# Latent cross-attentions: each slot's side work on PE in front of the transposes of the probabilities

## The chip, the cores and the metric

The kernel runs on one core of one Trainium2 chip. The metric is the device time of one execution in microseconds. The engines are called by their short names: PE (TensorE, matmuls and transposes), DVE (VectorE), ACT (ScalarE), POOL (GpSimd) and SP (SyncE). PSUM, in which PE's results land, has 8 banks of 128 x 512 float32.

## The reference

A decoder of four layers on x of 4 batches x 512 tokens x 256 features, float32. Each layer has an attention, a cross-attention and a feed-forward part. The change touches three of the four cross-attentions, those of layers 1, 2 and 3, in which the tokens are the latents that ask, and keys and values come from 64 context rows and from the tokens themselves. That of layer 2, cut to what matters:

```python
def _L2_xattn_ref(x, latents, mask, ...):      # HEADS = 16, DIM_HEAD = 64
    xn = layernorm(x, ln_x_g, ln_x_b)          # x: the context, 64 rows
    ln = layernorm(latents, ln_l_g, ln_l_b)    # latents: the tokens, 512 rows
    q = (ln @ Wq).reshape(b, m, h, d).transpose(0, 2, 1, 3)
    kv = jnp.concatenate([xn @ Wkv, ln @ Wkv], axis=1)
    kv = kv.reshape(b, n + m, 2, h, d)
    k = kv[:, :, 0].transpose(0, 2, 1, 3)
    v = kv[:, :, 1].transpose(0, 2, 1, 3)
    qn = rmsnorm(q, qn_g) * scale
    kn = rmsnorm(k, kn_g)
    sim = jnp.einsum('bhid,bhjd->bhij', qn, kn)
    sim = jnp.where(padded_mask[:, None, None, :], sim, max_neg)
    attn = jax.nn.softmax(sim.astype(jnp.float32), axis=-1).astype(sim.dtype)
    out = jnp.einsum('bhij,bhjd->bhid', attn, v)
    return out.transpose(0, 2, 1, 3).reshape(b, m, h * d) @ Wout + bout
```

Layer 1 has no rmsnorm, mask or bias and 16 heads too. Layer 3 has 8 heads, l2-normed queries and keys, a mask, and a layer norm behind the output projection.

## The kernel before, in words

The program is one after the other twelve stages, written engine by engine; each engine runs its own list of instructions in the order of the code, and semaphores are the only link between lists. The stages of layers 1, 2 and 3 that matter are one function, `latent_attention` (line 2158), called three times. Nothing in it is planned by a program: the order is written out by hand.

**Slots.** For each batch `b` of four, the engines run a loop over slots `s`. A slot is one tile of 128 tokens (t = s % 4) of one pair of heads (j = s // 4): 32 slots in a batch with 16 heads, 16 with 8 heads. Slot s computes these things, each on its engine:

- PE waits for the exponentials of the slot before and makes the scores, 128 x 576 for each of the two heads, into PSUM banks 0 to 3 (line 2463).
- DVE adds the mask where there is one (L2826), takes the negated row maxima of the two heads (L2830), copies the transposed probabilities of slot s - 2 out of PSUM (`copy_probs`, L2760, one copy for each head), does small work for the next batch, and at the start of the next slot's list inverts the sums (`invert`, L2751).
- ACT makes the exponentials with their sums (L2588), then moves results of side work and of the pair out of PSUM (L2546, L2551, L2557, L2561).
- POOL scales the probabilities by the inverted sums (`share`, L2630 for the two heads' 512 tokens, L2633 for the context part).
- PE transposes the scaled probabilities of slot s - 2 (LAG = 2), four 128 x 128 blocks for each head, into bank 4 or 5 in turn (`turn_probs`, L2392). In slots with s % 4 = 1 it also transposes the context part of a whole pair into one of the same two banks (`turn_context_probs`, L2404), and in slots with s % 4 = 2 and 3, from s = 6 on, it multiplies the transposed probabilities of a pair with the values (`attended`, L2422, L2425).

**Side work.** `units_at(b, s)` gives PE at most one further unit in a slot; all units write bank 7. `value` (L2327, 4 matmul instructions) projects a tile of values of this batch; `out_part` (L2339, 8 instructions) is half of an output projection of a tile of the batch before (in layer 3 a whole one); `turn_batch` (L2319, 4 transposes) turns the next batch's normed rows. For 16 heads the values sit at s = 0 to 5, 8, 9, 12, 13, the outputs at s = 16, 17, 20, 21, 24, 25, 28, 29 of batches 1 to 3, and the turns at 26 and 27; for 8 heads the values at 0 to 4, the outputs at 5, 8, 9, 12 and the turns at 14 and 15 (`norm_units`, line 2142). `bank_free` holds the waits of a unit for bank 7.

**The waits that matter.** `turn_context_probs` waits for POOL and for `copied` of 8q + 7 (q counts the pairs): DVE's copy of the first head of slot s - 2, whose transposes stand in this same slot and used the bank that the context transposes write:

```python
n = 9 * q + 8
pe.wait_ge(shared, 3 * (b * NS + s) + 3)
pe.wait_ge(copied, 8 * q + 7)
```

`turn_probs` waits for POOL's scaling of its slot and for the earlier copy out of each bank. ACT's exponentials of slot g wait for the transposes of slot g - 3 (three buffers of probabilities).

Between two batches there is a tail, in which the last transposes are mixed with the projections of queries and keys of the next batch; its code is not touched.

Of the kernel before, what the change touches and what calls it, by code (L numbers as in the profile page):

```python
# [2157 lines left out]
def latent_attention(k, pre, H, names, unit=None, mask=None, bias_row=None, gain_row=None, offset_row=None):  # L2158
# [16 lines left out]
    LAG = 2  # L2175
# [7 lines left out]
    with ExitStack() as st:  # L2183
# [38 lines left out]
        def units_at(b, s):  # L2222

            out = []
            if s in VALUES:
                out.append(("value", VALUES.index(s)))
            if s in OUTS and b >= 1:
                out.append(("out", OUTS.index(s)))
            if s in TURNS and b + 1 < B:
                out.append(("turn", TURNS.index(s)))  # L2230
            return out
# [18 lines left out]
        def units_before(b):  # L2250
            return N0 + b * NQ

        with signals(nc, "ctx_stat", "ctx_aggr", "ctx_shift", "ctx_rstd", "ctx_normed", "ctx_turned", "ctx_ready",
# [28 lines left out]
            def _(pe):  # L2282

                def bank_free(b, s, kind):

                    if kind == "value":
                        n = VALUES.index(s)
                        if n:
                            pe.wait_ge(value_moved, b * NV + n)
                            if n % (TT + 1) == 0:  # L2290
                                pe.wait_ge(ctx_value_moved, b * A + n // (TT + 1))
                    if kind == "out":
                        n = OUTS.index(s)
                        if n % PER_OUT:
                            return
                        if n == 0:
                            pe.wait_ge(value_moved, b * NV + NV)
                            pe.wait_ge(ctx_value_moved, b * A + A)
                        elif TURNS[-1] > OUTS[n - 1] and TURNS[-1] < s and b + 1 < B:
                            pe.wait_ge(norm_moved, KC * (b + 2))  # L2300
                        else:
                            pe.wait_ge(out_added, TT * (b - 1) + n // PER_OUT)
                    if kind == "turn":
                        n = TURNS.index(s)
                        if n:
                            pe.wait_ge(norm_moved, KC * (b + 1) + n)
                        else:
                            before = sum(o < s for o in OUTS)
                            if b >= 1:
                                pe.wait_ge(out_added, TT * (b - 1) + before // PER_OUT)  # L2310
                            else:
                                pe.wait_ge(value_moved, b * NV + NV)
                                pe.wait_ge(ctx_value_moved, b * A + A)

                def turn_batch(b, c):
                    if c == 0:
                        pe.wait_ge(normed, TT * (b + 1))
                    for t in range(TT):
                        last = pe.transpose(k.ps[:, 7, t * P:(t + 1) * P], xr[:, t, c * P:(c + 1) * P], k.ident[:, :])  # L2319
                    last.then_inc(norm_turned, 1)  # L2320

                def value(b, n):
                    t, a = n % (TT + 1), n // (TT + 1)
                    for c in range(KC):
                        rows = xT[:, c, t * P:(t + 1) * P] if t < TT else \
                            ctx2[:, c, b, :, :].rearrange("p s n -> p (s n)")
                        last = pe.matmul(k.ps[:, 7, :], rows, wkv[:, c, W + a * 512:W + (a + 1) * 512],  # L2327
                                         start=c == 0, stop=c == KC - 1)
                    last.then_inc(value_made, 1)
# [45 lines left out]
                def step(i, i0, i1):  # L2375
                    if i < i1:
                        project(i)
                    if unit and i0 <= i - 2 < i1:
                        turn_unit(i - 2)

                def turn_probs(b, s):
                    q, t = b * PAIRS + s // 4, s % 4
                    for h in range(2):
                        n = 9 * q + 2 * t + h
                        pe.wait_ge(shared, 3 * (b * NS + s) + 1 + h)
                        if n % 9 == 1 and q >= 1:
                            pe.wait_ge(ctx_copied, q)
                        elif n >= 2:
                            pe.wait_ge(copied, 8 * q + 2 * t + h - (2 if n % 9 >= 2 else 1) + 1)
                        at = 0 if h == 0 else T + 2 * NC  # L2390
                        for c in range(TT):
                            last = pe.transpose(k.ps[:, 4 + n % 2, c * P:(c + 1) * P],  # L2392
                                                prob[:, (b * NS + s) % PB, at + c * P:at + (c + 1) * P], k.ident[:, :])
                        last.then_inc(prob_turned, 1)
# [51 lines left out]
                for b in range(B):  # L2446
                    for s in range(NS):
                        g = b * NS + s
                        if s == 0:
                            if unit:  # L2450
                                pe.wait_ge(moved, units_before(b + 1))
                            else:
                                pe.wait_ge(act_moved, units_before(b + 1) // 2)
                                pe.wait_ge(dve_moved, units_before(b + 1) // 2)
                            pe.wait_ge(placed, 2 * (b + 1))
                        else:
                            pe.wait_ge(exped, 2 * g)
                        j, t = s // 4, s % 4
                        for a in range(2):
                            for h in range(2):  # L2460
                                r = slice(64 * h, 64 * h + 64)
                                k0 = (NC if h == 0 else 0) + a * HALF
                                last = pe.matmul(k.ps[:, 2 * h + a, 0:HALF], qT[r, b % 2, j, t * P:(t + 1) * P],  # L2463
                                                 kT[r, j, k0:k0 + HALF], start=True, stop=True)
                        last.then_inc(scored, 1)
                        if s >= LAG:
                            turn_probs(b, s - LAG)
                        for kind, n in units_at(b, s):
                            bank_free(b, s, kind)
                            if kind == "value":  # L2470
                                value(b, n)
                            elif kind == "out":
                                out_part(b - 1, n, 7)
                            else:
                                turn_batch(b + 1, n)
                        if s >= LAG:
                            turn_context_probs(b, s - LAG)
                        if s >= 4 + LAG and (s - 4 - LAG) % 4 < 2:
                            attended(b, (s - 4 - LAG) // 4, (s - 4 - LAG) % 4)
                    i0, i1 = units_before(b + 1), units_before(b + 2) if b + 1 < B else units_before(b + 1)  # L2480
                    turn_probs(b, NS - 2)
                    if b + 1 < B:
                        pe.wait_ge(norm_moved, KC * (b + 2))
                        pe.wait_ge(exped, 2 * NS * (b + 1))
                        if b:
                            pe.wait_ge(out_added, TT * b)
                        for i in range(i0, i0 + 3):
                            step(i, i0, i1)
                    turn_probs(b, NS - 1)
                    if b + 1 < B:  # L2490
                        step(i0 + 3, i0, i1)
                    turn_context_probs(b, NS - 1)
                    if b + 1 < B:
                        for i in range(i0 + 4, i0 + 6):
                            step(i, i0, i1)
                    attended(b, PAIRS - 1, 0)
                    attended(b, PAIRS - 1, 1)
                    if b + 1 < B:
                        for i in range(i0 + 6, i1 + 2):
                            step(i, i0, i1)  # L2500
# [2424 lines left out]
```

## Time and profile before

| what | value |
|---|---|
| median of 3 runs | 3956.74 us (3950.29 to 3959.68) |
| the profiled execution, its own time | 3976.31 us |
| its span | 3974.6 us |
| granted TensorE clock over the span | 0.928 |
| busy over the span: PE, DVE, ACT, POOL | 88%, 55%, 38%, 35% |
| first and last scores (L2463) | 655.5 and 3597.2 us |
| slots in layers 1, 2 and 3 | 128, 128, 64 |
| layer 1's scores | 655.6 to 1305 us |
| layer 2's scores | 2012 to 2720 us |
| layer 3's scores | 3224 to 3597 us |

A row of the page groups instructions by line of the code: busy time, mean duration of one, and the idle time of that engine right in front of them with what ended it. A row of a timeline is one instruction or a run of equal ones: its start, how long the run lasts, how many, and in brackets the idle time of the engine before it and the instruction that ended it. Matmuls overlap: a run's end is that of its last matmul, and the next may begin before. PEld are the loads of the stationary operand, which run beside other matmuls.

### The profile page before, as it was taken

What the parts mean: (1) busy time and instruction counts of PE and PEld (TensorE: products, weight loads), DVE (VectorE), ACT (ScalarE), POOL (GpSimd) and SP (SyncE); (2) the same over time, 40 slices, a digit from 0 to 9 for tenths busy, and PEclk for the clock granted to TensorE, in tenths of its full rate; (3) what the DMA queues carried; (4) which work ended last, traced back from release to release, by engine and by line L of the source; (5) the groups of instructions that cost most, each with busy time, mean ns of one, the idle gap of its engine ahead of it and who ended that gap; (6) DMA issues with size and microseconds to landing.
All of it is one profiled execution on the core that took longest, in us unless ns stands there. A gap on an engine that the chain in (4) does not pass through costs nothing. (4 is left out here: it accounts for less than half of the span.)

```text
span 3974.6 us, 54454 instructions
## 1 busy us (share of the span) xinstructions
PE 3504.1 (88%) x18930; PEld 2229.3 (56%) x18930; DVE 2171.8 (55%) x5265; ACT 1496.3 (38%) x3039; POOL 1395.8 (35%) x2006
## 2 busy tenths in 40 slices
PE   8998897899999877888798999998896779996997
PEld 5675684445555565344444555556792444554896
DVE  5374444645646477666366666664334356665454
ACT  3253203433434273233344444443351044442453
POOL 2142341422324164332344454543422144442311
PEclk9999978999999988899799999998898789997998
DMA  2005001000000000000100000002221000003212
GB/s 99 1 1 122 14 1 45 1 1 1 1 1 1 13 1 23 1 1 1 48 1 1 1 1 1 1 1 97 86 77 50 1 28 1 1 1 158 70 60 83
DMA packets 48719, 108.86 MB, mean 27 GB/s; under 512 B 6660, under 2 KB 32900, under 8 KB 46404
## 3 DMA queue, kind: packets, MB, share of 16 engines
q1 hardware_dynamic: 40964, 84.88, 6.4%
q0 software_dynamic: 7488, 20.49, 1.4%
q8 instruction: 158, 2.59, 0.3%
q14 instruction: 109, 0.89, 0.1%
HBM read 70.67 MB, written 34.68 MB: 27 GB/s over the span
## 5 line engine op out<-in xcount | busy, mean ns | idle before, releaser
L2630 POOL TENSOR_SCALAR probs<-probs,inv_sum 128x512 f32<-128x512 f32 x640 | 436.6, 695 | 964.1 <-DVE inv_sum L2751 963.8
L2588 ACT ACTIVATE probs<-psum_banks,neg_max 128x576 f32<-128x576 f32 x640 | 468.5, 737 | 712.0 <-DVE neg_max L2830 712.0
L2830 DVE TENSOR_REDUCE neg_max<-psum_banks 128x1 f32<-128x576 f32 x640 | 455.2, 753 | 192.8 <-PE psum_banks L2463 186.2
L2463 PE MATMUL psum_banks<-keys_T,queries_T 64*128 64x288 f32 x2560 | 407.4, 438 | 39.9 <-ACT probs L2588 27.7
L2760 DVE COPY probs_T<-psum_banks 128x512 f32<-128x512 f32 x640 | 409.5, 681 | 20.0 <-PE psum_banks L2392 20.0
L2463 PEld LDWEIGHTS psum_banks<-keys_T,queries_T 64*128 64x128 f32 x2560 | 225.5, 190 | 268.0 <-ACT probs L2588 160.6
L2392 PE MATMUL psum_banks<-ident,probs 128*128 128x128 f32 x2560 | 352.1, 281 | 3.2 <-POOL probs L2630 2.3
L2392 PEld LDWEIGHTS psum_banks<-ident,probs 128*128 128x128 f32 x2560 | 276.6, 141 | 130.4 <-POOL probs L2630 72.6
L2422 PE MATMUL psum_banks<-probs_T,values 128*64 128x512 f32 x1280 | 307.3, 604 | 2.2 <-issue 2.2
L4382 PE MATMUL psum_banks<-sorted_T,tile_weights 128*128 128x128 f32 x2208 | 271.7, 280 | 8.8 <-ACT tile_weights L4472 4.9
L4382 PEld LDWEIGHTS psum_banks<-sorted_T,tile_weights 128*128 128x128 f32 x2208 | 262.0, 197 | 11.6 <-issue 11.4
L4398 PE MATMUL psum_banks<-w_L_experts_down,hidden_T 128*128 x736 | 178.9, 387 | 18.6 <-DVE expert_rows L4656 15.0
L2826 DVE TENSOR_TENSOR psum_banks<-psum_banks,key_mask 128x128 f32<-128x128 f32 x192 | 57.5, 299 | 247.4 <-PE psum_banks L2463 247.4
L4285 POOL DMA_INDIRECT expert_outputs<-expert_rows,output_index x92 | 89.8, 976 | 291.6 <-DVE expert_rows L4659 124.3
L2645 POOL TENSOR_TENSOR square_sum<-square_sum,neg_half 128x8 f32<-128x8 f32 x102 | 169.3, 1660 | 8.5
L2327 PE MATMUL psum_banks<-w_L_xattn_Wkv,batch_normed_T 128*128 128x512 f32 x320 | 162.7, 633 | 0.0
L4398 PEld LDWEIGHTS psum_banks<-w_L_experts_down,hidden_T 128*128 128x128 f32 x736 | 135.3, 194 | 35.5 <-issue 20.3
L2422 PEld LDWEIGHTS psum_banks<-probs_T,values 128*64 128x64 f32 x1280 | 79.2, 136 | 126.6 <-issue 123.8
L4472 ACT COPY tile_weights<-w_L_experts_up 128x1024 f32 (+1 forms) x92 | 135.2, 1472 | 23.9 <-issue 23.7
L2726 DVE TENSOR_REDUCE square_sum<-squares 128x8 f32<-128x512 f32 x102 | 70.0, 686 | 129.5 <-ACT squares L2533 129.5
L1962 ACT ACTIVATE probs_T<-psum_banks 128x512 f32<-128x512 f32 (+3 forms) x128 | 83.0, 701 | 127.6 <-PE psum_banks L1899 126.6
L2633 POOL TENSOR_TENSOR context_probs<-probs,inv_sum 128x128 f32<-128x128 f32 x320 | 128.3, 401 | 0.0
(534 smaller groups left out, 6181.3 us busy)
## 6 DMA issues: line engine op xcount, KB each, us to landing
normed<-sorted_rows SPq DMA_DIRECT2D x30, 385.5 KB
sorted_rows<-zero_rows SPq DMA_DIRECT2D x8, 1028.0 KB, 16.4
w_L_experts_down<-in_L_experts_down SPq DMA_DIRECT2D x2, 4096.0 KB, 37.3
normed<-expert_outputs SPq DMA_DIRECT2D x8, 1024.0 KB, 7.8
w_L_xattn_Wkv<-in_L_xattn_Wkv SPq DMA_DIRECT2D x2, 2048.0 KB, 8.2
w_L_experts_up<-in_L_experts_up SPq DMA_DIRECT2D x1, 4096.0 KB, 12.3
sorted_rows<-zero_rows SPq DMA_DIRECT2D x4, 899.5 KB, 15.0
x_res<-in_x SPq DMA_DIRECT2D x4, 512.0 KB, 6.9
```

What stands on the lines that cost most here:

```text
L2327: last = pe.matmul(k.ps[:, 7, :], rows, wkv[:, c, W + a * 512:W + (a + 1) * 512], start=c == 0, stop=c == KC - 1)
L2392: last = pe.transpose(k.ps[:, 4 + n % 2, c * P:(c + 1) * P], prob[:, (b * NS + s) % PB, at + c * P:at + (c + 1) * P], k.ident[:, :])
L2422: last = pe.matmul(k.ps[r, 6, :], v[:, c, (2 * j + h) * 64:(2 * j + h + 1) * 64], pT[:, q % 2, h, c, :], start=c == 0, stop=False)
L2463: last = pe.matmul(k.ps[:, 2 * h + a, 0:HALF], qT[r, b % 2, j, t * P:(t + 1) * P], kT[r, j, k0:k0 + HALF], start=True, stop=True)
L2588: act.activation(prob[:, g % PB, h * w:(h + 1) * w].rearrange("p (a n) -> p a n", a=2), k.ps[:, 2 * h:2 * h + 2, 0:HALF], ACT.Exp, bias=nm ...
L2630: pool.tensor_scalar(w, w, inv[:, g % 4, h:h + 1], 1.0, ALU.mult, ALU.mult).then_inc(shared, 1)
L2645: pool.tensor_tensor(ss[:, i % 4, 2, :], ss[:, i % 4, 1, :], k.half[:, 0:8], ALU.pow).then_inc(inverted, 1)
L2760: dve.tensor_copy(pT[:, q % 2, h, :, t * P:(t + 1) * P], k.ps[:, 4 + n % 2, :].rearrange("p (c q) -> p c q", q=P)).then_inc(copied, 1)
L2830: dve.tensor_reduce(nmax[:, g % 4, h:h + 1], k.ps[:, 2 * h:2 * h + 2, 0:HALF], AX.XY, ALU.max, negate=True).then_inc(maxed, 1)
L4382: last = pe.matmul(ps[:, 2 * (n % 2) + part, f * P:(f + 1) * P], wt[:, n % 2, c, part * 512 + f * P:part * 512 + (f + 1) * P], xsT[:, n % ...
L4398: last = pe.matmul(ps[:, 6, 0:D], h[:, n % 2, f * P:(f + 1) * P], w_down[:, f // F, f % F * D:f % F * D + (E - 1) * STEP + D][:, bass.ds(a ...
L4472: act.copy(wt[:, n % 2, :, :], w_up[:, :, 0:(E - 1) * STEP + UP][:, :, bass.ds(at, UP)]).then_inc(weights_copied, 1)
```

## The change

In the loop over slots, PE's list is changed in one place, for all three stages: the block that makes the slot's unit of side work, with `bank_free`, is put in front of `turn_probs` instead of behind it. `turn_context_probs` and `attended` stay behind both. The lists of the other engines are the same as before.

```diff
--- before.py
+++ after.py
@@ -2463,8 +2463,6 @@
                                 last = pe.matmul(k.ps[:, 2 * h + a, 0:HALF], qT[r, b % 2, j, t * P:(t + 1) * P],
                                                  kT[r, j, k0:k0 + HALF], start=True, stop=True)
                         last.then_inc(scored, 1)
-                        if s >= LAG:
-                            turn_probs(b, s - LAG)
                         for kind, n in units_at(b, s):
                             bank_free(b, s, kind)
                             if kind == "value":
@@ -2473,6 +2471,8 @@
                                 out_part(b - 1, n, 7)
                             else:
                                 turn_batch(b + 1, n)
+                        if s >= LAG:
+                            turn_probs(b, s - LAG)
                         if s >= LAG:
                             turn_context_probs(b, s - LAG)
                         if s >= 4 + LAG and (s - 4 - LAG) % 4 < 2:
```

## Rows read from the trace of the kernel before

**Rows 1.** The page, costliest groups: line, engine, count | busy, mean ns | idle before, releaser

```profile
L2392 PE MATMUL psum_banks<-ident,probs 128*128 128x128 f32 x2560 | 352.1, 281 | 3.2 <-POOL probs L2630 2.3
L2392 PEld LDWEIGHTS psum_banks<-ident,probs 128*128 128x128 f32 x2560 | 276.6, 141 | 130.4 <-POOL probs L2630 72.6
L2630 POOL TENSOR_SCALAR probs<-probs,inv_sum 128x512 f32<-128x512 f32 x640 | 436.6, 695 | 964.1 <-DVE inv_sum L2751 963.8
L2633 POOL TENSOR_TENSOR context_probs<-probs,inv_sum 128x128 f32<-128x128 f32 x320 | 128.3, 401 | 0.0
```

**Rows 2.** Busy time in stretches: PE, PEld, DVE, ACT, POOL, then PE clock

```profile
826.00:1310.00 484.00, 478.54 (x2528) 264.15 (x2528) 280.65 (x533) 203.16 (x485) 167.20 (x290) 1.00 0.00 1
2121.00:2152.00 31.00, 27.18 (x140) 16.26 (x140) 18.66 (x39) 12.85 (x31) 10.46 (x19) 0.78 0.00 1
2210.00:2716.00 506.00, 491.42 (x2597) 270.24 (x2595) 330.46 (x660) 227.91 (x524) 232.63 (x359) 0.99 0.00 1
```

**Rows 3.** Timeline of PE, layer 1, batch 1, s = 4 and 5: start, us, what

```profile
841.82 1.24 PE L2463 MATMUL psum_banks<-keys_T,queries_T 64*128 64x288 f32 x8
843.92 1.88 PE L2327 MATMUL psum_banks<-w_L_xattn_Wkv,context_T_twice 128*128 128x512 f32 x4
845.74 1.24 PE L2463 MATMUL psum_banks<-keys_T,queries_T 64*128 64x288 f32 x8
846.91 1.09 PE L2392 MATMUL psum_banks<-ident,probs 128*128 128x128 f32 x8
847.84 1.88 PE L2327 MATMUL psum_banks<-w_L_xattn_Wkv,batch_normed_T 128*128 128x512 f32 x4
849.56 0.60 PE L2404 MATMUL psum_banks<-ident,context_probs 128*128 128x128 f32 x4
850.09 0.51 PE L2463 MATMUL psum_banks<-keys_T,queries_T 64*128 64x288 f32 x2
```

**Rows 4.** Timelines of DVE and ACT in the same slot s = 5

```profile
847.02 1.42 DVE L2830 TENSOR_REDUCE neg_max<-psum_banks 128x1 f32<-128x576 f32 x2 [1.22 <-PE psum_banks L2463]
848.36 1.28 DVE L2760 COPY probs_T<-psum_banks 128x512 f32<-128x512 f32 x2
...
845.84 0.76 ACT L2561 COPY context_values<-psum_banks 64x256 f32<-64x256 f32 x2 [0.38 <-PE psum_banks L2327]
```

**Rows 5.** Timeline of PE, layer 1, batch 1, s = 1, which has no transposes

```profile
830.31 1.24 PE L2463 MATMUL psum_banks<-keys_T,queries_T 64*128 64x288 f32 x8 [0.52 <-ACT probs L2588]
831.48 1.98 PE L2327 MATMUL psum_banks<-w_L_xattn_Wkv,batch_normed_T 128*128 128x512 f32 x4
834.00 0.51 PE L2463 MATMUL psum_banks<-keys_T,queries_T 64*128 64x288 f32 x2 [0.53 <-ACT probs L2588]
```

**Rows 6.** Timeline of PE, layer 3, batch 1, scores of s = 8 and s = 9

```profile
3361.11 1.24 PE L2463 MATMUL psum_banks<-keys_T,queries_T 64*128 64x288 f32 x8
...
3365.14 1.24 PE L2463 MATMUL psum_banks<-keys_T,queries_T 64*128 64x288 f32 x8
```

**Rows 7.** Timelines of PE and DVE, layer 1, batch 0, s = 17, without a unit

```profile
730.08 0.63 PE L2404 MATMUL psum_banks<-ident,context_probs 128*128 128x128 f32 x4 [1.19 <-DVE probs_T L2760]
730.64 0.51 PE L2463 MATMUL psum_banks<-keys_T,queries_T 64*128 64x288 f32 x2
...
729.26 1.28 DVE L2760 COPY probs_T<-psum_banks 128x512 f32<-128x512 f32 x2
```

**Rows 8.** Timeline of DVE, layer 3, batch 1, s = 8

```profile
3362.74 1.42 DVE L2830 TENSOR_REDUCE neg_max<-psum_banks 128x1 f32<-128x576 f32 x2
...
3365.28 0.41 DVE L2768 COPY projected<-psum_banks 128x256 f32<-128x256 f32 x1
...
3365.94 0.15 DVE L2751 RECIPROCAL inv_sum<-exp_sum 128x2 f32<-128x2 f32 x1
```

**Rows 9.** Timeline of PE, layer 2, batch 0, s = 17, without a unit

```profile
2089.91 0.63 PE L2404 MATMUL psum_banks<-ident,context_probs 128*128 128x128 f32 x4 [1.52 <-DVE probs_T L2760]
```

**Rows 10.** Groups by line, PE, 655 to 1310 us: busy, mean ns | idle before

```profile
L2404 PE MATMUL psum_banks<-ident,context_probs 128*128 128x128 f32 x124 | 18.7, 273 | 4.8 <-DVE probs_T L2760 4.8
```

## The prediction

> **What bounds the kernel now.** I read the page first, then the two helper lines that the change swaps, then single slots in order of time. A slot is one pass of the loop over s in `latent_attention`. The page shows TensorE as the busiest engine, and in front of the matmuls that transpose the probabilities (L2392) it shows 3.2 us of idle time in 2560 of them; the 130.4 us in the row below stand before the weight loads of the same line, which run beside other matmuls [rows 1]. So PE hardly ever waits before those transposes. Between 826 and 1310 us, three of the four batches of layer 1's cross-attention, PE is busy for 478.5 of 484 us at a granted clock of 1.00, while DVE is busy for 280.7 [rows 2]. The masked layer 2 looks alike, 491.4 of 506 [rows 2].
>
> The slots repeat to 0.01 us, so one of each kind stands for all. A slot has a floor, the **chain** scores, row maxima, exponentials, next scores: 3.69 us without a mask (830.31 to 834.00, where PE sits idle 0.53 us for ACT) [rows 5] and 4.02 to 4.03 us with one (3361.11 to 3365.14) [rows 6]. A plain slot with a unit is set by PE's own work in layer 1: scores to transposes 1.17, transposes to unit 0.93, unit to next scores 1.81 or 1.82, together 3.92 (841.82 to 845.74) [rows 3]. Every fourth slot (s%4 = 1) also transposes the context probabilities (L2404): 1.17 + 0.93 + 1.72 (unit to L2404) + 0.53 (L2404 to scores) = 4.35 us (845.74 to 850.09) [rows 3]. That is above both floors, so anything added to PE there counts in full.
>
> **The change, part by part.** Nothing is added or removed; 8 transposes and one unit (1.88 us) change places. The scores, the unit's own operands and the waits stay.
>
> *PE order alone.* Directly behind the scores a unit lasts 1.98 instead of 1.88 [rows 3, 5]; its hand-over to a transpose takes 1.72 [rows 3], so the transposes of the probabilities start at 1.17 + 1.72 + 0.10 = 2.99 us into the slot instead of 1.17. Four transposes take 0.53 from their start to the next scores, and four more add some 0.43 (8 in 1.09 less 4 in 0.60, with the surplus of a first one, 0.06, off) [rows 3]: 0.96. A plain unit slot becomes 3.95 to 3.96, 0.04 more than 3.92, in layer 1 alone: 8 value slots of s = 2, 3, 12 of s = 4, 8, 12 and 12 output slots, 32 x 0.04 = **1.3 us**. In the masked layers 3.96 is hidden under the chain's 4.02 [rows 6]; that cover is 0.06 thick.
>
> *The context slot.* The code lets L2404 start only when DVE has copied out the first head's transposes, since both use one PSUM bank. Today DVE does that copy at 848.36, right after its maxima, and it is over before PE has finished the unit: hidden. After the change the first head is turned at 2.99 + 0.60 = 3.59 us; DVE starts a copy about 0.05 behind (scores end 846.98, maxima start 847.02) [rows 3, 4], at 3.64. What comes then is shown by the context slots that have no unit, where PE does wait: copy starts 729.26, L2404 starts 730.08 with 1.19 us of idle before it, the scores follow at 730.64, hence 0.82 + 0.56 [rows 7]. The new slot is 3.64 + 0.82 + 0.56 = 5.02 us against 4.35, or **0.67 us** more. DVE is free by then in the masked layers too: its maxima end at 3362.74 + 1.42, 3.05 into a slot that began at 3361.11 [rows 6, 8]. How many: s = 5, 9, 13 carry values in all four batches and s = 17, 21, 25, 29 outputs in three, 12 + 12 = 24 in layer 1, 24 in layer 2; layer 3 has half the slots, and s = 5, 9 carry outputs in three batches: 6. 54 x 0.67 = **36.2 us**. Bounds: if the wait were wholly covered by the order of PE's work, the slot would be 3.96 + 0.44 = 4.40, or 0.04 more, 2 us in all; if DVE started its copy 0.1 later than I take, 54 x 0.1 = 5.4 more.
>
> *What queues behind.* On DVE the two copies now lie at 3.64 to 4.92 and the reciprocal after them, until 5.0. In a plain slot of layer 1 the next scores are complete at 3.96 + 1.24 + 0.05 = 5.25 and in the masked ones at 5.31, so the next maxima aren't held; the cover is some 0.25. It is used up where DVE has more to do in a plain unit slot. In layer 3 at s = 8 and 12 it also copies the projection out (copy to reciprocal 0.66 with the statistics of the next batch) [rows 8]: reciprocal at 4.84 + 0.66 = 5.50, its end 5.6 against 5.3, so 0.3 in the slot after s = 12 in two batches; behind s = 8 the slot is PE's, but its unit waits for that copy until 5.30 instead of 5.19: 0.11 x 3. Together **0.9 us**. GpSimd scales a slot's probabilities behind the reciprocal, 1.0 us later than today: from about 5.1, two of 0.70 and one of 0.40 [rows 1], over at 6.9; they are needed by the transposes two slots on, at 2 x 3.96 + 1.17 = 9.1 at the earliest: nothing. ACT moves a unit's result out after its exponentials either way, over at 0.76 + 0.10 of the next slot [rows 4], in front of the next unit at 1.17: nothing, though 0.3 is all there is. The slots that carry `attended` have no unit, or one of transposes of 0.53 in a PE-bound slot: nothing. SP's and POOL's queues are not passed. The tails between batches are not touched.
>
> *The clock.* The granted clock is 1.00 in stretches whose slots have 0.53 us of idle at their end, and fell to 0.78 once, in the one stretch of layer 2 where slots without units idle 1.5 us before L2404 [rows 2, 5, 9]. My new idle time, 0.43 us in one slot of four, is of the first kind; I take no cost. The Trainium skill speaks against me: "TensorE: Matmul & The Clock Gate", section "A second HAM failure mode: psum-queue depth-cycling", says that short idle times between groups of matmuls that cycle through PSUM banks can set the clock swinging between its levels. By that the sum would be rival 3's, by the rows it stays.
>
> Sum: 1.3 + 36.2 + 0.9 = 38.4 us. The profiled execution took 3976.3 us (span 3974.6); with the change about 4014.7. The runs shown have a median of 3956.7, 19.6 below it; the addition is the same, so 3956.7 + 38.4 = **3995.1 us**.
>
> **Rivals.** (1) *The wait is covered, no change.* The copy's start would have to be hidden behind the unit as today. Against: the code's count names the copy of this very slot. Gives +1.3 to +2, 3958. 4 in 100. (2) *Faster: the unit fills a wait for GpSimd.* 72.6 us of idle are put down to GpSimd's scaled probabilities before L2392's loads [rows 1]. If PE truly waited there, up to 72.6 would go, and with the 36.2 still paid it ends at 3920. It decides if GpSimd's result comes later than 1.17 us into the slot. Against: the matmul row, 3.2 us in all, of which GpSimd 2.3. 2 in 100. (3) *The clock falls in unit slots.* The stretch 2121 to 2152 ran at 0.78 [rows 2]: of its 31 us, 0.22/0.5 x 31 = 13.6 were at 1.2 GHz, costing at most 6.8. Once in each of the 11 batches that have such slots would be up to 75 us, 4070; once or twice more than today, 4002 to 4009. 12 in 100, nearly all of it at once or twice. The skill's rule named above is this one; the trace agrees only for longer idle times. It can also go the other way: the one fall there is today sits in a stretch that the change only shifts in time, and may vanish, minus 6.8.
>
> **How the numbers follow.** The forecast has 82 in 100. Its own range: the copy's start 0 to +0.1 later gives 0 to +5.4, the hand-over +-0.05 in 54 slots +-2.7, one fall of the clock more or less +-6.8, and medians of three runs of this kernel move by some 5. Taken together about -10 to +14: 3985 to 4009. Rivals 1, 2 and the far end of 3 stay outside. A measurement of this kernel can tell about 0.2%, 8 us; every case but the first two lies above +8: slower 0.94, same 0.04, faster 0.02.
>
> **What would show it.** Right: L2404 idles about 0.43 us in each of the 54 slots for DVE's copy, about 15 us in layer 1 instead of 4.8 [rows 10]; context slots with a unit take 5.02; plain ones in layer 1 3.96; masked plain ones stay at 4.02; all three stages grow, by about 17.5, 16 and 5 us. Wrong, if context slots stay under 4.5, if plain slots grow by more than 0.1 (then DVE holds the maxima), or if the granted clock of 826 to 1310 falls below 0.98.

## The result and the profile after

| | before | changed |
|---|---|---|
| median, first measurement (4 runs each) | 3954.6 us | 4001.3 us (3998.6 to 4003.6) |
| ratio, with its 95% interval | | 1.0119 (1.0105 to 1.0133) |
| ratio, measured again (experiment e4) | | 1.0101 (1.0086 to 1.0115) |
| profiled execution, own time | 3976.3 us | 4000.0 us |
| layer 1, first to last scores | 649.8 us | 667.4 us (664.1 to 1331.5) |
| layer 2, first to last scores | 707.8 us | 719.8 us (2039.3 to 2759.1) |
| layer 3, first to last scores | 372.5 us | 377.9 us (3247.1 to 3625.0) |

The change makes the kernel slower by 1.0 to 1.2%: +46.7 us in the first measurement, +40 in the second. The forecast was +38.4 us and 3995.1, with a range of 3985 to 4009. The two profiled executions differ by only 23.7 us, because the one of before was 20 us above its median. The stages themselves grew by 17.6 + 12.0 + 5.4 = 35.0 us. The rest lies in code that the change does not touch: the changed kernel's execution took 16.0 us less between layers 2 and 3 (488.1 against 504.1) and 4.7 less behind layer 3, 1.0 more between layers 1 and 2, and it came to layer 1 8.5 us later (664.1 against 655.6).

The context slot first. This is the timeline of PE in the changed kernel, layer 1, batch 1, s = 4 and 5, the same two slots as [rows 3] (start, us, what, and in brackets idle time and what ended it):

```profile
852.67 1.24 PE L2463 MATMUL psum_banks<-keys_T,queries_T 64*128 64x288 f32 x8
853.84 1.98 PE L2327 MATMUL psum_banks<-w_L_xattn_Wkv,context_T_twice 128*128 128x512 f32 x4
855.66 1.04 PE L2392 MATMUL psum_banks<-ident,probs 128*128 128x128 f32 x8
856.63 1.24 PE L2463 MATMUL psum_banks<-keys_T,queries_T 64*128 64x288 f32 x8
857.80 1.98 PE L2327 MATMUL psum_banks<-w_L_xattn_Wkv,batch_normed_T 128*128 128x512 f32 x4
859.62 1.04 PE L2392 MATMUL psum_banks<-ident,probs 128*128 128x128 f32 x8
861.10 0.63 PE L2404 MATMUL psum_banks<-ident,context_probs 128*128 128x128 f32 x4 [0.44 <-DVE probs_T L2760]
861.65 0.51 PE L2463 MATMUL psum_banks<-keys_T,queries_T 64*128 64x288 f32 x2
```

The plain slot lasts 3.96 us (852.67 to 856.63), the context slot 5.02 (to 861.65), and L2404 has got 0.44 us of idle time that [rows 3] do not have. Its releaser is DVE's copy. The timeline of DVE in the same stretch shows that copy, which answers to [rows 4]:

```profile
856.91 0.68 DVE L2760 COPY probs_T<-psum_banks 128x512 f32<-128x512 f32 x1
857.50 0.15 DVE L2751 RECIPROCAL inv_sum<-exp_sum 128x2 f32<-128x2 f32 x1
857.92 1.42 DVE L2830 TENSOR_REDUCE neg_max<-psum_banks 128x1 f32<-128x576 f32 x2 [0.26 <-PE psum_banks L2463]
860.26 1.29 DVE L2760 COPY probs_T<-psum_banks 128x512 f32<-128x512 f32 x2 [0.92 <-PE psum_banks L2392]
861.46 0.15 DVE L2751 RECIPROCAL inv_sum<-exp_sum 128x2 f32<-128x2 f32 x1
```

DVE has its maxima done at 859.34 and then idles 0.92 us until PE has turned the first head; before, the copy began at once. The second copy and the reciprocal of the plain slot lie behind the slot's end at 856.63 (856.91, 857.50), and the next maxima still find DVE free, with 0.26 us to spare.

The groups by line of PE, changed kernel, 664 to 1336 us (layer 1; busy, mean ns | idle before):

```profile
L2392 PE MATMUL psum_banks<-ident,probs 128*128 128x128 f32 x1008 | 134.1, 276 | 0.0
L2404 PE MATMUL psum_banks<-ident,context_probs 128*128 128x128 f32 x124 | 19.4, 279 | 15.3 <-DVE probs_T L2760 14.4 <-POOL context_probs L2633 0.9
```

L2404's idle time went from 4.8 us [rows 10] to 15.3, which is 24 x 0.44 more. The 0.9 us put down to GpSimd are two of these slots, 5.03 and 5.04 us long like their neighbours. There GpSimd ends a result of the next tile in the same moment as DVE its copy; the one that L2404 needs had been done for 7 us. The transposes of the probabilities idle 0.0 us: nothing was gained in front of them, as nothing was there. The page of the changed kernel has the same 3.2 us for the whole run as [rows 1]. Below are the row of DVE's copies before, the same row after the change, and the row of the transposes after it:

```profile
L2760 DVE COPY probs_T<-psum_banks 128x512 f32<-128x512 f32 x640 | 409.5, 681 | 20.0 <-PE psum_banks L2392 20.0
L2760 DVE COPY probs_T<-psum_banks 128x512 f32<-128x512 f32 x640 | 410.3, 682 | 119.5 <-PE psum_banks L2392 119.4
L2392 PE MATMUL psum_banks<-ident,probs 128*128 128x128 f32 x2560 | 342.7, 277 | 3.2 <-POOL probs L2630 2.3
```

It is now DVE that waits for PE's transposes: 119.5 us in front of its copies, where it was 20.0. Most of that costs nothing; what costs is the one copy in every fourth slot that PE waits for in turn.

### The profile page after: what moved, and what is told of

Same layout as the page of the kernel before. It is cut to its first block and busy times, and to the rows that moved or that the text cites. A ratio compares the mean times of both kernels' runs of the same rounds, so it can differ in the third digit from the quotient of the medians.

```text
span 3998.3 us, 54454 instructions
## 1 busy us (share of the span) xinstructions
PE 3521.7 (88%) x18930; PEld 2241.8 (56%) x18930; DVE 2182.4 (55%) x5265; ACT 1488.7 (37%) x3039; POOL 1392.2 (35%) x2006
## 5 line engine op out<-in xcount | busy, mean ns | idle before, releaser
L2760 DVE COPY probs_T<-psum_banks 128x512 f32<-128x512 f32 x640 | 410.3, 682 | 119.5 <-PE psum_banks L2392 119.4
L2392 PEld LDWEIGHTS psum_banks<-ident,probs 128*128 128x128 f32 x2560 | 287.7, 141 | 117.2 <-issue 59.9
L2392 PE MATMUL psum_banks<-ident,probs 128*128 128x128 f32 x2560 | 342.7, 277 | 3.2 <-POOL probs L2630 2.3
```

Of the source, the lines that this page charges most:

```text
L2392: last = pe.transpose(k.ps[:, 4 + n % 2, c * P:(c + 1) * P], prob[:, (b * NS + s) % PB, at + c * P:at + (c + 1) * P], k.ident[:, :])
L2760: dve.tensor_copy(pT[:, q % 2, h, :, t * P:(t + 1) * P], k.ps[:, 4 + n % 2, :].rearrange("p (c q) -> p c q", q=P)).then_inc(copied, 1)
```

## The experiments

All kernels compute the same thing as the kernel before; only the order of PE's list or a wait differs.

**e1 and e2: the change in two halves.** e1 makes the unit first only in slots with context transposes, e2 only in the others.

```diff
-                        if s >= LAG:
+                        if s >= LAG and s % 4 != 1:
                             turn_probs(b, s - LAG)
                         for kind, n in units_at(b, s):
...
+                        if s >= LAG and s % 4 == 1:
+                            turn_probs(b, s - LAG)
                         if s >= LAG:
                             turn_context_probs(b, s - LAG)
```

(e1; in e2 the two conditions change places.)

> The unit stands in front of the transposes only in the slots with s%4 = 1, which also carry the context transposes; all other slots are as before. Theory (the wait of L2404 for DVE's copy is the whole cost): 54 slots of 5.02 us instead of 4.35, +36 to +37 us against the kernel before, or nearly all of the measured +46.7 less an unexplained 8 to 10. Rival A (the plain slots carry the missing 8 to 10 us, by copies and reciprocals that come late): also +36 to +37 here, and the rest in the other half. Rival B (the missing 8 to 10 us hang on the context slots): +45 to +47 here.

> The other half: the unit stands in front of the transposes in all slots but those with s%4 = 1. Theory: +1 to +3 us against the kernel before, no change that can be measured; plain unit slots of layer 1 3.96 us, masked ones 4.02, context slots 4.35. Rival A: +8 to +10 us. Rival B: +1 to +3 us.

Measured: e1 has a ratio of 1.0092 (1.0076 to 1.0108), which on the 3982.9 us of the kernel before is +36.6, with an interval of 30 to 43; e2 1.0011 (1.0000 to 1.0023), +4.4 with an interval of 0 to 9. The two halves add to 41, e4 below gives 40. PE's timeline of e2, s = 4 and 5 of layer 1, batch 1:

```profile
843.24 1.24 PE L2463 MATMUL psum_banks<-keys_T,queries_T 64*128 64x288 f32 x8
844.41 1.98 PE L2327 MATMUL psum_banks<-w_L_xattn_Wkv,context_T_twice 128*128 128x512 f32 x4
846.23 1.04 PE L2392 MATMUL psum_banks<-ident,probs 128*128 128x128 f32 x8
847.20 1.24 PE L2463 MATMUL psum_banks<-keys_T,queries_T 64*128 64x288 f32 x8
848.37 1.09 PE L2392 MATMUL psum_banks<-ident,probs 128*128 128x128 f32 x8
849.30 1.88 PE L2327 MATMUL psum_banks<-w_L_xattn_Wkv,batch_normed_T 128*128 128x512 f32 x4
851.02 0.60 PE L2404 MATMUL psum_banks<-ident,context_probs 128*128 128x128 f32 x4
851.55 0.51 PE L2463 MATMUL psum_banks<-keys_T,queries_T 64*128 64x288 f32 x2
```

The changed plain slot takes 3.96 us, the context slot that follows it is back at 4.35 with no idle time, although DVE's late copy of the plain slot reaches into it. So late copies as such cost nothing here, and nine tenths of the cost hang on the 54 context slots. Rival B wanted +45 to +47, and e1 ends at +43 at most. Rival A's +8 to +10 lies at the edge of e2's interval, so the times alone do not exclude it; the stages of e2's own profile do not show it: layer 1 is 1.4 us longer than before, layer 3 0.2 longer and layer 2 0.2 shorter. In one place late work on DVE does cost: in layer 3 the slots s = 9 and s = 13 take 4.58 or 4.59 us in two batches each instead of 4.35 or 4.36. There DVE also carries the projection and work for the next batch out of the slot before, and the mask of the next scores is added with no idle time of DVE in front of it.

**e3: the heads apart.** PE transposes the first head, makes the unit, transposes the second.

```diff
-                def turn_probs(b, s):
+                def turn_probs(b, s, heads=(0, 1)):
...
-                    for h in range(2):
+                    for h in heads:
...
                         if s >= LAG:
-                            turn_probs(b, s - LAG)
+                            turn_probs(b, s - LAG, (0,))
                         for kind, n in units_at(b, s):
...
+                        if s >= LAG:
+                            turn_probs(b, s - LAG, (1,))
```

> In every slot with a unit PE transposes the first head, then makes the unit, then transposes the second head. The context transposes need the copy of the first head alone, which is early again, while the second head's copy and the reciprocal behind it stay about 1 us later than before. Theory: context slots with a unit 4.35 to 4.39 us, L2404 idle for DVE only in slots without a unit, total 0 to +3 us against the kernel before. Rival (what costs is that DVE's copies and reciprocals come late as such, not this one wait): +15 us or more, context slots between 4.6 and 5.0.

Measured: 1.0002 (0.9991 to 1.0014), +1 us. PE's timeline of e3 in s = 5, then DVE's (its copies are L2762 in this kernel, the reciprocal L2753):

```profile
847.21 1.24 PE L2463 MATMUL psum_banks<-keys_T,queries_T 64*128 64x288 f32 x8
848.38 0.66 PE L2392 MATMUL psum_banks<-ident,probs 128*128 128x128 f32 x4
848.87 1.88 PE L2327 MATMUL psum_banks<-w_L_xattn_Wkv,batch_normed_T 128*128 128x512 f32 x4
850.59 0.60 PE L2392 MATMUL psum_banks<-ident,probs 128*128 128x128 f32 x4
851.03 0.60 PE L2404 MATMUL psum_banks<-ident,context_probs 128*128 128x128 f32 x4
851.56 0.51 PE L2463 MATMUL psum_banks<-keys_T,queries_T 64*128 64x288 f32 x2
```

```profile
849.83 0.68 DVE L2762 COPY probs_T<-psum_banks 128x512 f32<-128x512 f32 x1
851.23 0.69 DVE L2762 COPY probs_T<-psum_banks 128x512 f32<-128x512 f32 x1 [0.71 <-PE psum_banks L2392]
851.84 0.16 DVE L2753 RECIPROCAL inv_sum<-exp_sum 128x2 f32<-128x2 f32 x1
```

The first head's copy is early again (849.83, right behind the maxima), L2404 follows without idle time, and the slot is 4.35 us. The second copy starts 4.02 us into the slot and the reciprocal 4.63, against 4.23 and 4.83 in the changed kernel and 3.22 and 3.82 in the kernel before: both stay late, and cost nothing. This is the clearest of the runs: half of the reordering is kept and the whole cost is gone, because the one copy that something waits for is early.

**e4: the changed kernel again**, five executions, on the chip of e1 to e3.

> The changed kernel again, five rounds on this chip beside the kernel before, to narrow the size: by the slots of its profile +38 us; by the first measurement +46.7 (interval 41.5 to 52.6). If 38 and the difference is scatter, the ratio lies between 1.008 and 1.011; if something outside the slots adds 8 us, it lies between 1.0115 and 1.0125.

Measured: 1.0101 (1.0086 to 1.0115), +40 us on 3982.9. Both kernels took 21 to 28 us longer in this measurement than in the first. The slots of its profile repeat those of the changed kernel: 5.02 to 5.04 us for a context slot with a unit in layers 1 and 2, 3.96 or 3.97 for a plain unit slot of layer 1. In layer 3 two slots s = 14 differ: 6.12 us instead of 4.62, at a granted clock of 0.76 (3426 to 3433), which makes that stage 380.6 us instead of 377.9. So two executions of one kernel can differ by 3 us in a stage, by where the clock falls. The ratio lies in the band I had named for scatter, 1.008 to 1.011. But its interval and that of the first measurement overlap only between 1.0105 and 1.0115, so a few us beside the slots are not excluded.

**e5: a longer wait.** The changed kernel, with L2404 waiting for the second head's copy as well.

```diff
-                    pe.wait_ge(copied, 8 * q + 7)
+                    pe.wait_ge(copied, 8 * q + 8)
```

> The changed kernel, in which the context transposes wait for DVE's copy of the second head too (8 instead of 7 in the count). DVE starts the second copy 0.60 us behind the first. Theory: each of the 54 context slots with a unit goes from 5.02 to 5.62, in all +32 us against the changed kernel, plus some 0.6 in each of the 16 or so context slots without a unit, +10, together +42: about +88 us against the kernel before. Rival (the slot is set by PE's order or by the late reciprocal, not by this copy): +46 as the changed kernel.

Measured: 1.0221 (1.0204 to 1.0238), +87 us on 3957.2. PE's timeline of e5, s = 5:

```profile
854.61 1.24 PE L2463 MATMUL psum_banks<-keys_T,queries_T 64*128 64x288 f32 x8
855.78 1.98 PE L2327 MATMUL psum_banks<-w_L_xattn_Wkv,batch_normed_T 128*128 128x512 f32 x4
857.60 1.04 PE L2392 MATMUL psum_banks<-ident,probs 128*128 128x128 f32 x8
859.67 0.63 PE L2404 MATMUL psum_banks<-ident,context_probs 128*128 128x128 f32 x4 [1.04 <-DVE probs_T L2760]
860.23 0.51 PE L2463 MATMUL psum_banks<-keys_T,queries_T 64*128 64x288 f32 x2
```

The idle time grows from 0.44 to 1.04 and the slot from 5.02 to 5.62: 0.60 us, the distance of two copies on DVE, comes out in full.

**e6: no late copy, but no cover.** The kernel before, with the context transposes in front of the unit.

```diff
                             turn_probs(b, s - LAG)
+                        if s >= LAG:
+                            turn_context_probs(b, s - LAG)
                         for kind, n in units_at(b, s):
...
-                        if s >= LAG:
-                            turn_context_probs(b, s - LAG)
```

> The kernel before, in which the context transposes stand right behind the transposes of the probabilities and the unit last. Nothing is late on DVE; only the unit no longer covers the copy. Theory: L2404 starts 3.45 us into a slot of layer 1 and 3.79 into a masked one, the unit 0.43 later and the next scores 1.81 after that: 5.70 and 6.04 us instead of 4.35, 24 x 1.35 + 30 x 1.69 = +83 us against the kernel before. Rival (what the change costs comes from DVE's late copies): 0 here, since the copies keep their place.

Measured: 1.0208 (1.0191 to 1.0225), +82 us. PE's timelines of e6 in s = 5 of layer 1 and of layer 2:

```profile
858.04 1.24 PE L2463 MATMUL psum_banks<-keys_T,queries_T 64*128 64x288 f32 x8
859.21 1.09 PE L2392 MATMUL psum_banks<-ident,probs 128*128 128x128 f32 x8
861.50 0.63 PE L2404 MATMUL psum_banks<-ident,context_probs 128*128 128x128 f32 x4 [1.19 <-DVE probs_T L2760]
861.96 1.88 PE L2327 MATMUL psum_banks<-w_L_xattn_Wkv,batch_normed_T 128*128 128x512 f32 x4
863.77 0.51 PE L2463 MATMUL psum_banks<-keys_T,queries_T 64*128 64x288 f32 x2
...
2275.89 0.63 PE L2404 MATMUL psum_banks<-ident,context_probs 128*128 128x128 f32 x4 [1.53 <-DVE probs_T L2760]
```

The slot takes 5.73 us (5.70 forecast), and L2404 idles 1.19 us, as in the slots without a unit [rows 7], 1.53 in layer 2, as in [rows 9]. Here DVE's copies follow its maxima at once, as in the kernel before. So the copy always ends later than PE's transposes of the probabilities; what the kernel before has is a unit standing between the two transposes, 1.72 us from its start to L2404 [rows 3], and that is what hides it.

## Why the prediction was right

*PE does not wait in front of L2392.* Right: its idle time is 3.2 us in both kernels. The 72.6 us of the weight loads [rows 1] were no waiting of PE, and rival 2 (faster) had nothing to take. Rival 1 (the wait is covered) falls with the 0.44 us in front of L2404.

*The context slot, 0.67 us in each of 54, 36.2 us.* Right to 0.01 us: 4.35 to 5.02 with values. Slots with an output unit take 5.03 to 5.04 instead of 4.36, the same 0.67. The idle time in front of L2404 is 0.44 (0.43 forecast), 15.3 us in layer 1 (about 15). As a part by itself, e1 gives +36.6. The step behind it, that DVE's copy of the same slot is what counts, is shown by e3, e5 and e6 from three sides.

*PE's order alone, 1.3 us.* Right in the slots of layer 1: 3.96 with values and 3.97 with outputs, 1.6 us in the 32 of them; the masked ones stay at 4.02. e2's time (+4.4, 0 to 9) is too coarse to confirm 1.3.

*What queues behind, 0.9 us.* In layer 3 the context slot behind s = 8 takes 5.15 to 5.16 us, 0.12 above the others; 0.11 was forecast. The slot behind s = 12 takes 4.58 instead of 4.35 in two batches, 0.23 more; 0.3 was forecast. GpSimd and ACT stayed covered: the plain slots have the length that PE's own order gives them.

*By stages.* 17.5, 16 and 5 us were forecast, 17.6, 12.0 and 5.4 came. Layer 2 is short by 4 us, and the granted clock is the cause: the stretch in which it had fallen, batch 0 from s = 25 on, ran at 0.78 before [rows 2]. The same slots of the changed kernel (first row; busy time in a stretch: PE, PEld, DVE, ACT, POOL, then the granted clock) ran at 1.00. The second row is the changed kernel's layer 1. The third is batch 1 of layer 2 in e6:

```profile
2146.00:2180.00 34.00, 27.44 (x178) 15.91 (x180) 22.67 (x48) 14.33 (x34) 13.77 (x24) 1.00 0.00 1
840.00:1336.00 496.00, 481.97 (x2516) 266.18 (x2516) 281.72 (x531) 200.34 (x485) 166.37 (x290) 1.00 0.00 1
2257.00:2395.00 138.00, 126.16 (x714) 71.72 (x712) 90.14 (x188) 58.60 (x142) 53.10 (x92) 1.00 0.00 1
```

Layer 2's 24 context slots with a unit give 16.2 us. So this step was right in the slots and missed a gain of 4.3 us that the text had only allowed for as a possibility. Layer 3's 5.4 us hold 1.0 us of another fall, in slot s = 9 of batch 0 (5.31 us instead of 4.35).

*Rival 3, a clock that falls in unit slots.* It did not happen: 1.00 over 840 to 1336, with the new 0.44 us gap in every fourth slot, and none of the 54 context slots is lengthened by it. It did not even happen in e6, where the unit slots of layer 2 idle 1.53 us: 1.00 over 2257 to 2395. The working had also taken the fall of before for the only one. Its trace has one more at each start of batches 1 to 3 in layers 2 and 3 (0.95 over 2152 to 2210), and so has that of the changed kernel. The Trainium skill ("TensorE: Matmul & The Clock Gate", section "A second HAM failure mode: psum-queue depth-cycling") says that short idle times between groups of matmuls can make the clock swing between its levels. The trace does not show that in the slots with a unit, at gaps of 0.44 to 1.53 us. The falls of before between s = 25 and 30 came in a stretch whose slots have no unit of values or outputs; in such slots PE idles 1.52 us in front of L2404 at full clock [rows 9].

*The size.* 38.4 us were forecast, 46.7 and 40 measured. The forecast ratio of 1.0097 lies inside the second interval and just below the first. The sum over the stages of the two profiles is 35.0. Taken slot by slot, without those in which the clock fell in either profile, the growth is 36.4 in the 54 context slots, 1.6 in the plain ones of layer 1 and 0.8 behind s = 8 and 12 of layer 3: 38.8 us. What the first measurement has beyond that, some 8 us, was not found in any slot. It may lie ahead of them, where the two kernels are the same: the profile of the changed kernel comes to layer 1 8.5 us later, and 5.8 of these arise between 185 and 221 us, where its granted clock is lower (the same matmul starts at 185.0 and 184.9 us, one 120 further on at 215.4 and 221.1). Before, then changed:

```profile
190.00:230.00 40.00, 32.60 (x235) 24.70 (x236) 30.70 (x82) 18.64 (x31) 16.81 (x20) 0.91 0.00 1
190.00:230.00 40.00, 33.03 (x185) 23.76 (x185) 25.81 (x71) 15.99 (x26) 14.56 (x18) 0.74 0.00 1
```

e6's profile has the same 0.74 there, those of e1 and e5 have 0.91, and e4, the same kernel as the changed one, came to layer 1 at 658.7 us. So this is a difference between executions. Whether the other executions of the first measurement had it is not on record, and nothing here settles the last few us.

## What to carry to other kernels

When a step on an in-order engine is moved back, ask what its result sets going on another engine, and whether something later in the same pass needs that back again. Here the transposes start DVE's copy and the context transposes need its bank, so the unit between them was the cover for a wait of 1.19 us, 1.53 with a mask (e6). In front of both it leaves 0.44 us of wait open. Its own place in the order was worth almost nothing (1.6 us in all plain slots). If a reorder is wanted all the same, keep the one piece that somebody waits for early (e3: the first head) and let the rest be late.

The idle time in front of the weight loads (130.4 us here) was no waiting of PE (3.2 us), and the change, which put work in front of those transposes, found nothing to fill: look at the matmul row of the same line before hoping for a gain.

## What had not been expected of the hardware

In every profile the granted clock falls in the second half of batch 0 of layer 2, but not in the same slots. From s = 16 on, this batch has no unit but the two turns at s = 26 and 27. Slot s = 26 took 6.20, 6.16, 6.19 and 5.92 us in the profiles of the kernel before, e2, e3 and e5, and 4.50 us, at full clock, in those of the changed kernel, e1, e4 and e6. But these four have a fall too, only earlier. In the changed kernel, e1 and e4 it is at s = 17 (5.06, 5.01 and 5.07 us instead of 4.35), in e6 at s = 21 (5.27 instead of 4.35). This is the changed kernel around s = 17:

```profile
2113.00:2121.00 8.00, 5.60 (x31) 3.78 (x31) 6.15 (x13) 4.17 (x10) 2.06 (x4) 0.79 0.00 0
```

In e2 and e3 the slots ahead of it last as long as before, while in the changed kernel, e1, e4 and e6 the context slots ahead are longer. e5 has longer slots too and has both falls, at s = 18 (5.69 instead of 4.06) and from s = 25 on. So slot length alone does not decide it; what does stays open. The later fall is worth 4.3 us (s = 25 to 30 take 31.1 us with it, 26.8 without), the earlier one 0.7 to 0.9.
